# A three-stage block on one core: who makes the inputs of the state scan

## The chip, the core and the metric

The kernel runs on one core of a Trainium2 chip. The metric is the device time of one execution in microseconds (us). The engines named below are TensorE (PE in the profile; PEld is its weight load), VectorE (DVE), ScalarE (ACT), GpSimd (POOL) and SyncE (SP), which here only issues DMAs. All of them work through their own instruction list in order and wait for each other through semaphores. A change within about 0.3% can't be told from no change here.

## The reference, cut to what matters

`x` has 16 batches of 512 tokens with 256 features, all float32. Each batch goes through four residual stages: causal attention with 16 heads of 16 features, a feed-forward layer with a small router over 6 experts, a state-space layer, and the same feed-forward layer again.

```python
x = x + attn(layernorm(x), ...)
x = x + ffn(layernorm(x), ...)
x = x + ssm(layernorm(x), ...)
x = x + ffn(layernorm(x), ...)
```

The state-space layer is where the change is made. Per feature `d` and state `n` (16 states) it runs a recurrence over the 512 tokens:

```python
delta = softplus(xc @ Wd.T + bd);  Bm = xc @ Wb.T;  Cm = xc @ Wc.T
decay = exp(A * dt);  inp = dt * xt * bt     # per state n
h = decay * h + inp
y = sum over n of h * ct
```

## The kernel before, in words

A batch is held with features on the 128 partitions in two halves (C = 2 halves of 128 features) and the 512 tokens along the free dimension. With `u = dt * xc` (both halves, 128x1024), state `n` of batch `s` takes one step of this kind:

- SyncE loads row `n` of B, which lies in DRAM as `b_kept`, broadcast to 128 partitions, into one of three places of `b_all` (`load_b`, L759 on). It waits until `inputs` of three steps earlier is done.
- ScalarE makes `dec` with two exponentials (`decays`).
- GpSimd makes `inp` (`inputs`, L1325 on) with two multiplications of 128x512, one per half: L1333 for half 0, L1339 for half 1, both from `u` and `b_all` in SBUF. `dec` and `inp` have two places each, so `inputs` of step `n` waits for scan `n-2`.
- VectorE runs the recurrence over both halves as one scan of 128x1024 (`scan`, L1164), and then `product` (L1172) multiplies the state by row `n` of C, which TensorE has spread over a PSUM bank (`spread_bank`).
- GpSimd adds the product to `y` by a DMA with addition (`add_state`, L1346). For the last two batches TensorE adds in PSUM instead (`sum_y`, L596).

Only in the last batch is it otherwise already: there TensorE spreads row `n` of B over `pv_bank` (L585), VectorE makes half 1 from it directly behind the scan before (`half_of_inputs`, L1145), and GpSimd makes half 0 alone.

Beside these steps VectorE takes the maxima of the attention scores from two PSUM banks (L1030, L1033, L1035; 40 of them in each batch), normalises heads (L1057, L1059), adds residuals (L1080, L1088), makes silu (L1128), `dt` and `u` (L1136, L1138), the gated y (L1178) and the router (L1096 to L1122). TensorE makes the scores twice (L392, L394 for the maxima; L415, L417 for the exponentials), the products with the values (L440) and all projections.

The order of work is written out by hand. Each engine loops over `now` from START to STOP; a batch has a frame of 80 slots. The tables PE_AT, ACT_AT, DVE_AT, POOL_AT and SP_AT give for each piece of work the slot, counted from its batch's frame, at which an engine takes it up; `due` turns a slot into a batch. A slot is a place in an engine's list and no time: what an engine does is set by the order and the waits. All batches have the same places. Several batches are under way at once, since a batch runs from slot -114 to slot 285 of its frame: the scans of one batch lie beside the attention of a batch two frames later. The last two batches' scans therefore lie behind the end of the attention work.

On each engine the work beside the scans keeps its place in the loop: on VectorE a slot's maximum comes first, then `side_work`, then scans, then products.

Of the kernel before, what the change touches and what calls it, by code (L numbers as in the profile page):

```python
# [56 lines left out]
def hybrid_block(nc, x, norm_w, wqk_t, bqk_c, wv_t, bv, wo_t, bo, conv_w, conv_b, wd_t, bd, wbc_t,  # L57
# [37 lines left out]
    PE_AT = {"res": (-29, -34), "xn": (-76, -74), "qk00": (-55, -51, -47), "qk01": (-47, -45, -43),  # L95
# [6 lines left out]
             "sum": (165, 177, 182, 189, 189, 192, 200, 209, 211, 211, 219, 224, 224, 232, 235, 242)}  # L102
    BANK = {"res": (1, 1), "xn": (0, 0), "qk00": 0, "qk01": 1, "v": (1, 0), "qk10": 0, "qk11": 1, "ao": (0, 1),
            "x1": (1, 1), "turn0": (1, 1), "low0": 1, "hw0": 0, "up0": (0, 1), "xs": (0, 1), "conv": (0, 1),
            "gate": (0, 1), "bc": 1, "dt": (0, 0), "x3": (1, 0), "turn1": (0, 1), "low1": 1, "hw1": 0, "up1": (0, 1)}
    ACT_AT = {"res": (-28, -34), "square_f": 100, "square_s": 124, "square_l": 251, "norm_f": 103, "norm_s": 129,
# [5 lines left out]
              "decays": (154, 165, 169, 170, 170, 176, 187, 190, 197, 197, 204, 216, 218, 219, 219, 225)}  # L112
    DVE_AT = {"gated": 249, "add_x3": (250, 251), "in0": 112, "in1": 265, "out0": 116, "out1": 271,
              "add_up1": (277, 277), "add_x1": (92, 97), "add_up0": (122, 124), "silu": 140, "delta": 153,
              "stats_q": -114, "finish": -7, "heads": 26,
              "scan": (158, 169, 169, 171, 181, 183, 191, 195, 200, 204, 210, 217, 219, 224, 225, 227),
              "product": (161, 170, 174, 178, 182, 186, 194, 198, 201, 209, 215, 217, 222, 225, 232, 235)}
    POOL_AT = {"rsqrt_f": 91, "rsqrt_s": 128, "rsqrt_q": -110, "rsqrt_l": 241, "low": (116, 262),
               "inputs": (147, 152, 152, 152, 162, 167, 180, 180, 196, 204, 205, 210, 220, 221, 221, 225),
               "add": (160, 152, 165, 174, 180, 185, 191, 202, 205, 209, 214, 220, 221, 225, 225, 227)}  # L120
    SP_AT = {"parts": (-41, 1), "load_x": -112, "store_b": 151, "store": 285, "stack": (-29, -30, -29), "maxima": -4,
             "load_b": (152, 155, 156, 164, 169, 169, 175, 180, 194, 199, 208, 208, 211, 215, 215, 227)}
    ctx = ExitStack()
    with ctx:
# [115 lines left out]
        def has(b):  # L240
            return 0 <= b < NB
# [4 lines left out]
        def due(now, at):  # L246

            a, rest = divmod(now - at, FRAME)
            return a if rest == 0 and has(a) else -1

        def group(now, at):

            g, rest = divmod(now - at, HALF)
            return g if rest == 0 and 0 <= g < NQ else -1
# [65 lines left out]
        def _(pe):  # L320
# [257 lines left out]
            def spread_b(s, n):  # L578

                if s == NB - 1:  # L580
                    if n == 0:
                        pe.wait_ge(heads_done.sem, heads_done.at(NQ - 1))
                        pe.wait_ge(side["bc"].free, side["bc"].at("bc", s, 2))
                    pe.wait_ge(b_used.sem, b_used.at(0, n))
                    mm(pv_bank[:, :], onehot[:, n:n + 1].to_broadcast([3 * NC, P]), bcs[:, s % 2, :],  # L585
                       start=True, stop=True).then_inc(b_ready.sem, 1)
# [116 lines left out]
        def _(sp):  # L703
# [317 lines left out]
        def _(dve):  # L1021
# [118 lines left out]
            def half_of_inputs(n):  # L1140

                if n == 0:
                    dve.wait_ge(u_done.sem, u_done.at(NB - 1))
                dve.wait_ge(b_ready.sem, b_ready.at(0, n + 1))
                V.tensor_tensor(inp[:, n % 2, 1, :], pv_bank[:, :], u[:, 1, :], ALU.mult).then_inc(b_used.sem, 1)  # L1145

            def scan(s, n):
                k = NS * s + n
                old_s, old_n = divmod(k - HC, NS)
                if s == NB - 1 and n == 0:  # L1150
                    half_of_inputs(0)
# [13 lines left out]
                if s == NB - 1 and n + 1 < NS:  # L1165
                    half_of_inputs(n + 1)
# [125 lines left out]
        def _(pool):  # L1292
# [142 lines left out]
```

## Time and profile before

| | us |
|---|---|
| median of three runs | 2019.69 |
| lowest and highest of them | 2017.47, 2022.86 |
| the profiled execution, its own time | 2012.02 |
| its span from first to last instruction | 2010.2 |
| VectorE busy in the span | 1697.4 |
| TensorE busy in the span | 1791.8 |
| GpSimd busy in the span | 1163.8 |

The profile page gives busy time of each engine and groups of instructions. A group's line has its line number, engine, operation, what it writes and reads with shapes, the count, and behind the bar its busy time with the mean in ns; behind the next bar the idle time of that engine just before the group and what ended it. Busy time of an engine in a stretch counts overlapping instructions once. The answer by stretch of time gives the same busy times for any stretch, and the timeline lists one engine's instructions in order: start, duration, line. The duration of an instruction that is held while it runs contains the hold.

### The profile page before, as it was taken

The page shows a single profiled execution, that of the slowest core. Times are in us where ns is not written, and L with a number is a line of the kernel's source. Part 1 is how long each engine was busy: PE and PEld are TensorE (multiplying, and loading weights), DVE is VectorE, ACT ScalarE, POOL GpSimd, SP SyncE. Part 2 cuts the span into 40 slices and gives each one's busy share as a digit, 9 for nine tenths or more (in the row PEclk, how much of TensorE's full clock was granted, in tenths as well). Part 3 has the DMA queues.
Part 4 walks back from the last instruction along what each step waited for, and adds up shares of the span by engine and source line. Part 5 has one row for each costly group of instructions (what it writes and reads, how often), then busy time and mean ns, then how long its engine had stood idle before and what let it go on. Part 6 is the DMA issues. An engine that isn't in the chain of part 4 may idle for free.

```text
span 2010.2 us, 33547 instructions
## 1 busy us (share of the span) xinstructions
PE 1791.8 (89%) x11380; PEld 1109.9 (55%) x11380; DVE 1697.4 (84%) x2584; ACT 1408.9 (70%) x2724; POOL 1163.8 (58%) x933
## 2 busy tenths in 40 slices
PE   5889898999899898989999998999999898878775
PEld 3456464646566564746556565646565564535333
DVE  4444789999898989989999999989899999977783
ACT  2465768787785868777786968687886868675531
POOL 2000556676676666676676666666667666667430
PEclk9899989999999999999999999999999999989887
DMA  4322477766767676767768776866768776641110
GB/s 121 90 65 59 110 163 155 179 149 156 160 142 172 148 172 154 171 146 155 165 142 179 163 171 147 179 147 161 158 146 176 158 167 142 148 102 56 40 58 10
DMA packets 186091, 275.41 MB, mean 137 GB/s; under 512 B 33809, under 2 KB 125762, under 8 KB 185922
## 3 DMA queue, kind: packets, MB, share of 16 engines
q1 hardware_dynamic: 155682, 163.17, 31.5%
q0 software_dynamic: 30240, 110.11, 29.1%
q8 instruction: 91, 1.49, 0.3%
q14 instruction: 78, 0.64, 0.1%
HBM read 128.49 MB, written 34.08 MB: 81 GB/s over the span
## 4 chain that ended last, share of the span: by engine, by line
PE 36%; DVE 17%; DMA 15%; ACT 12%; issue 8%; POOL 7%; SPq 4%; POOLq 0%; DVEq 0%; ACTq 0%
PE bank L331 8%; DVE hc L1164 6%; DMA y<-hc 5%; PE bank L538 5%; DMA sk<-qk_parts 5%; SPq L748 3%; POOL inp L1333 3%; DMA out<-X 3%; PE bank L392 3%; PE bank L415 3%; PE bank L341 2%; PE bank L440 2%; PE bank L596 2%; POOL inp L1339 2%; PE bank L325 2%
## 5 line engine op out<-in xcount | busy, mean ns | idle before, releaser
L1164 DVE TENSOR_TENSOR_SCAN hc<-dec,inp 128x1024 f32<-128x1024 f32 x256 | 647.1, 2535 | 44.6 <-POOL inp L1339 13.8
L1333 POOL TENSOR_TENSOR inp<-u,b_all 128x512 f32<-128x512 f32 x256 | 445.9, 1742 | 207.2 <-DVE hc L1164 102.0
L812 ACT ACTIVATE pt<-bank 128x512 f32<-128x512 f32 x640 | 378.1, 596 | 121.8 <-PE bank L417 118.3
L1339 POOL TENSOR_TENSOR inp<-u,b_all 128x512 f32<-128x512 f32 x240 | 387.0, 1612 | 18.8
L928 ACT ACTIVATE dec<-dt,a_neg 128x511 f32<-128x511 f32 x512 | 340.1, 719 | 53.3 <-DVE hc L1164 53.3
L1346 POOL DMA_DIRECT2D y<-hc x210 | 185.5, 883 | 304.2 <-DMA y<-hc 196.2
L392 PE MATMUL bank<-sk,sq 96*128 96x512 bf16 (+3 forms) x1024 | 272.7, 305 | 49.1 <-DMA sk<-qk_parts 34.3
L1172 DVE TENSOR_TENSOR hc<-hc,bank 128x1024 f32<-128x1024 f32 x242 | 293.1, 1211 | 16.6 <-PE bank L575 15.5
L415 PE MATMUL bank<-sq,sk 98*128 98x512 bf16 (+3 forms) x1024 | 271.1, 303 | 8.0 <-ACT pt L812 7.5
L1033 DVE TENSOR_REDUCE mall<-bank 128x1 f32<-128x512 f32 x256 | 173.7, 678 | 62.2 <-PE bank L394 62.1
L1035 DVE TENSOR_REDUCE mall<-bank 128x4 f32<-128x512 f32 x256 | 173.7, 678 | 44.8 <-PE bank L394 44.8
L394 PE MATMUL bank<-mask_qk,ident_bf 128*128 128x128 bf16 x1024 | 194.5, 222 | 0.0
L417 PE MATMUL bank<-mask_kq,ident_bf 128*128 128x128 bf16 x1024 | 194.3, 221 | 0.0
L392 PEld LDWEIGHTS bank<-sk,sq 96*128 96x128 bf16 x1024 | 100.9, 99 | 158.6 <-issue 44.6
L440 PE MATMUL bank<-pt,v_sb 128*32 128x512 f32 (+3 forms) x2048 | 179.3, 446 | 0.8 <-ACT pt L812 0.8
L845 ACT ACTIVATE parts<-bank,bqk 128x512 bf16<-128x512 f32 x192 | 130.2, 688 | 42.6 <-PE bank L331 28.2
L331 PE MATMUL bank<-xt_q,wqk 128*128 128x512 f32 x256 | 125.4, 613 | 16.6 <-ACT bcs L908 15.8
L415 PEld LDWEIGHTS bank<-sq,sk 98*128 98x128 bf16 x1024 | 101.5, 99 | 68.0 <-ACT pt L812 17.4
L394 PEld LDWEIGHTS bank<-mask_qk,ident_bf 128*128 128x128 bf16 x1024 | 101.6, 99 | 45.9 <-issue 26.5
L1311 POOL TENSOR_TENSOR rs<-va,half 128x4 f32<-128x4 f32 x64 | 69.8, 1091 | 88.1 <-DVE ng L1075 84.0
L417 PEld LDWEIGHTS bank<-mask_kq,ident_bf 128*128 128x128 bf16 x1024 | 101.8, 99 | 31.4 <-issue 22.6
L575 PE MATMUL bank<-bcs,onehot 96*128 96x512 bf16 x256 | 98.9, 386 | 20.5 <-DVE hc L1172 20.4
(171 smaller groups left out, 3416.0 us busy)
## 6 DMA issues: line engine op xcount, KB each, us to landing
y<-hc POOLq DMA_DIRECT2D x210, 512.0 KB, 5.4
b_all<-b_kept SPq DMA_DIRECT2D x256, 256.0 KB, 4.4
qk_parts<-parts SPq DMA_DIRECT2D x96, 256.0 KB, 3.2
sq<-qk_parts SPq DMA_DIRECT2D x384, 64.0 KB, 3.7
sk<-qk_parts SPq DMA_DIRECT2D x384, 64.0 KB, 3.8
X<-in_x SPq DMA_DIRECT2D x16, 512.0 KB, 7.7
out<-X SPq DMA_DIRECT2D x16, 512.0 KB, 5.2
sq<-hlt SPq DMA_DIRECT2D x256, 2.0 KB
```

Of the source, the lines that this page charges most:

```text
L331: last = mm(dst[:, :], w[:, c, g * P:(g + 1) * P], src[:, c, :], start=(c == 0), stop=(c == C - 1))
L392: mm(dst[:, o:o + n], sq[0:KS, slot, h, qb * P:(qb + 1) * P], sk[0:KS, slot, h, 0:n], start=True, stop=False)
L394: return mm(dst[:, o + n - P:o + n], ident_bf[:, :], mask_qk[:, :], start=False, stop=True)
L415: mm(dst[:, o:o + n], sk[:, slot, h, kb * P:(kb + 1) * P], sq[:, slot, h, kb * P:T], start=True, stop=False)
L417: return mm(dst[:, o:o + P], ident_bf[:, :], mask_kq[:, :], start=False, stop=True)
L440: last = mm(pv_bank[VW * i:VW * (i + 1), kb * P:T], values_of(a, kb, first + i), pt[:, n % PT, at:at + T - kb * P], start=start, stop=stop ...
L812: A(pt[:, n % PT, :], score_bank[unit % 2][:, :], ACT.Exp).then_inc(exp_done.sem, 1)
L928: last = A(dec[:, n % 2, c, 1:T], dt[:, c, 1:T], ACT.Exp, scale=a_neg[:, c, n:n + 1])
L1164: V.tensor_tensor_scan(h, d, v, 0.0, ALU.mult, ALU.add).then_inc(scan_done.sem, 1)
L1172: V.tensor_tensor(hc[:, k % HC, :, :] if n or s >= LATE else y[:, s % 2, :, :], hc[:, k % HC, :, :], spread_bank[:, None, :].to_broadcast( ...
L1333: first = G.tensor_tensor(inp[:, n % 2, 0, :], u[:, 0, :], b_all[:, k % 3, :], ALU.mult)
L1339: G.tensor_tensor(inp[:, n % 2, 1, :], u[:, 1, :], b_all[:, k % 3, :], ALU.mult).then_inc(inp_ready.sem, 1)
```

## The change

VectorE makes half 1 of `inp` in every batch, not only in the last. In batches 0 to 14 it reads the row of B from `b_all` in SBUF, the same place that GpSimd reads for half 0; the last batch still takes it from `pv_bank`. It stands, as before in the last batch, directly behind the scan before it. GpSimd keeps half 0 only. The scan waits for both. `load_b` waits for both readers of the place that it fills. All places in the five tables are new, and batch 0, batch 14 and batch 15 get tables of their own (OWN), chosen by KIND in `due`. The numbers of operations other than the moved half are unchanged, and BANK gets a few other assignments.

```diff
+    KIND = [1 if a == 0 else max(a - NB + 4, 0) if a >= NB - 2 else 0 for a in range(NB)]
...
         def due(now, at):
-            a, rest = divmod(now - at, FRAME)
-            return a if rest == 0 and has(a) else -1
+            for kind, place in enumerate(at):
+                a, rest = divmod(now - place, FRAME)
+                if rest == 0 and has(a) and kind == KIND[a]:
+                    return a
+            return -1
...
                 sp.wait_ge(inp_ready.sem, inp_ready.at(old_s, old_n + 1))
+                sp.wait_ge(b_used.sem, b_used.at(old_s, old_n + 1))
...
-            def half_of_inputs(n):
+            def half_of_inputs(s, n):
+                k = NS * s + n
                 if n == 0:
-                    dve.wait_ge(u_done.sem, u_done.at(NB - 1))
-                dve.wait_ge(b_ready.sem, b_ready.at(0, n + 1))
-                V.tensor_tensor(inp[:, n % 2, 1, :], pv_bank[:, :], u[:, 1, :], ALU.mult).then_inc(b_used.sem, 1)
+                    dve.wait_ge(u_done.sem, u_done.at(s))
+                if s == NB - 1:
+                    dve.wait_ge(b_ready.sem, b_ready.at(0, n + 1))
+                    rows = pv_bank[:, :]
+                else:
+                    dve.wait_ge(b_loaded[k % 3].sem, b_loaded[k % 3].at(k // 3))
+                    rows = b_all[:, k % 3, :]
+                V.tensor_tensor(inp[:, n % 2, 1, :], rows, u[:, 1, :], ALU.mult).then_inc(b_used.sem, 1)
...
-                if s == NB - 1 and n == 0:
-                    half_of_inputs(0)
+                if n == 0:
+                    half_of_inputs(s, 0)
...
-                if s == NB - 1:
-                    dve.wait_ge(b_used.sem, b_used.at(0, n + 1))
+                dve.wait_ge(b_used.sem, b_used.at(s, n + 1))
...
-                if s == NB - 1 and n + 1 < NS:
-                    half_of_inputs(n + 1)
+                if n + 1 < NS:
+                    half_of_inputs(s, n + 1)
...
-                first = G.tensor_tensor(inp[:, n % 2, 0, :], u[:, 0, :], b_all[:, k % 3, :], ALU.mult)
-                if s == NB - 1:
-                    first.then_inc(inp_ready.sem, 1)
-                else:
-                    first.then_inc(pool_own.sem, 1)
-                    pool.wait_ge(pool_own.sem, pool_own.one())
-                    G.tensor_tensor(inp[:, n % 2, 1, :], u[:, 1, :], b_all[:, k % 3, :], ALU.mult).then_inc(inp_ready.sem, 1)
+                G.tensor_tensor(inp[:, n % 2, 0, :], u[:, 0, :], b_all[:, k % 3, :], ALU.mult).then_inc(inp_ready.sem, 1)
```

Of the tables, the rows of the usual batches for scans, products, inputs and loads of B:

```diff
-              "scan": (158, 169, 169, 171, 181, 183, 191, 195, 200, 204, 210, 217, 219, 224, 225, 227),
-              "product": (161, 170, 174, 178, 182, 186, 194, 198, 201, 209, 215, 217, 222, 225, 232, 235)}
+              "scan": (157, 167, 170, 171, 179, 184, 190, 194, 201, 204, 210, 216, 219, 223, 228, 230),
+              "product": (163, 170, 174, 178, 182, 189, 195, 199, 201, 207, 215, 218, 221, 225, 231, 236)}
...
-               "inputs": (147, 152, 152, 152, 162, 167, 180, 180, 196, 204, 205, 210, 220, 221, 221, 225),
+               "inputs": (142, 152, 152, 152, 164, 167, 176, 184, 193, 194, 201, 202, 214, 218, 218, 221),
...
-             "load_b": (152, 155, 156, 164, 169, 169, 175, 180, 194, 199, 208, 208, 211, 215, 215, 227)}
+             "load_b": (152, 152, 154, 165, 165, 172, 181, 185, 190, 198, 201, 207, 211, 212, 212, 213)}
```

## Rows read from the trace of the kernel before

**Rows 1.** The page: span, and the engines' busy time, share and instruction count.

```profile
span 2010.2 us, 33547 instructions
...
PE 1791.8 (89%) x11380; PEld 1109.9 (55%) x11380; DVE 1697.4 (84%) x2584; ACT 1408.9 (70%) x2724; POOL 1163.8 (58%) x933
```

**Rows 2.** Busy time by stretch: length, PE, PEld, DVE, ACT, POOL, clock, DMA.

```profile
0.00:213.50 213.50, 174.70 (x1170) 104.76 (x1170) 94.94 (x249) 109.75 (x205) 18.53 (x34) 0.96 0.30 83
213.50:1782.90 1569.40, 1450.57 (x9640) 912.21 (x9640) 1445.37 (x2154) 1207.42 (x2343) 1049.92 (x830) 0.99 0.72 158
1782.90:2010.20 227.30, 166.48 (x570) 92.98 (x570) 157.10 (x183) 91.69 (x178) 95.33 (x69) 0.86 0.16 46
```

**Rows 3.** Groups of VectorE instructions between 213.5 and 1782.9 us.

```profile
L1164 DVE TENSOR_TENSOR_SCAN hc<-dec,inp 128x1024 f32<-128x1024 f32 x224 | 568.1, 2544 | 36.1 <-ACT dec L928 11.0 <-issue 10.5 <-POOL inp L1339 10.2
L1172 DVE TENSOR_TENSOR hc<-hc,bank 128x1024 f32<-128x1024 f32 x209 | 253.1, 1211 | 3.0 <-PE bank L575 2.1
L1035 DVE TENSOR_REDUCE mall<-bank 128x4 f32<-128x512 f32 x220 | 149.0, 677 | 26.6 <-PE bank L394 26.6
L1033 DVE TENSOR_REDUCE mall<-bank 128x1 f32<-128x512 f32 x219 | 148.1, 676 | 14.4 <-PE bank L394 14.3
L1030 DVE TENSOR_REDUCE mall<-bank 128x2 f32<-128x512 f32 x110 | 74.6, 678 | 7.6 <-PE bank L394 7.6
L1088 DVE SCALAR_TENSOR_TENSOR X<-bank,X 128x256 f32<-128x256 f32 x164 | 62.4, 418 | 7.9 <-PE bank L522 7.9
...
L1128 DVE SCALAR_TENSOR_TENSOR xc<-sp_t,xc 128x1024 f32<-128x1024 f32 x14 | 22.9, 1634 | 0.4 <-ACT xc L891 0.4
...
L1138 DVE TENSOR_TENSOR u<-dt,xc 128x1024 f32<-128x1024 f32 x14 | 17.1, 1225 | 0.5
```

**Rows 4.** Waits of VectorE from 1782.9 us to the end: total us, times, longest.

```profile
DVE red L1096 <- ACT low L871: 14.0, 1, 14.0
DVE X L1080 <- PE bank L522: 13.6, 5, 8.0
```

**Rows 5.** Timeline of VectorE in the last batch: start, duration, instruction.

```profile
1951.32 0.67 DVE L1145 TENSOR_TENSOR inp<-bank,u 128x512 f32<-128x512 f32 x1
1951.90 1.21 DVE L1172 TENSOR_TENSOR hc<-hc,bank 128x1024 f32<-128x1024 f32 x1
```

**Rows 6.** Groups of GpSimd instructions between 213.5 and 1782.9 us.

```profile
L1333 POOL TENSOR_TENSOR inp<-u,b_all 128x512 f32<-128x512 f32 x224 | 393.8, 1758 | 154.1 <-DVE hc L1164 70.9 <-DVE u L1138 67.0 <-POOL inp L1339 9.5
...
L1346 POOL DMA_DIRECT2D y<-hc x208 | 183.7, 883 | 294.8 <-DMA y<-hc 194.8 <-DVE hc L1172 78.1 <-issue 10.9
```

**Rows 7.** GpSimd's second multiplication: count, ns min/median/max, first and last start.

```profile
L1339 POOL TENSOR_TENSOR inp<-u,b_all x240: 1261/1272/3346, 216.1 to 1873.4; 128x512 f32<-128x512 f32 x120
```

**Rows 8.** Timeline around 637 us: one scan of VectorE, two multiplications of GpSimd.

```profile
637.43 3.31 DVE L1164 TENSOR_TENSOR_SCAN hc<-dec,inp 128x1024 f32<-128x1024 f32 x1 [0.77 <-ACT dec L928]
...
637.03 1.55 POOL L1333 TENSOR_TENSOR inp<-u,b_all 128x512 f32<-128x512 f32 x1
638.66 3.16 POOL L1339 TENSOR_TENSOR inp<-u,b_all 128x512 f32<-128x512 f32 x1
```

**Rows 9.** Timeline around 1795 us: VectorE, then GpSimd; x2 merges two scans.

```profile
1794.75 1.53 DVE L1178 SCALAR_TENSOR_TENSOR y<-gate,y 128x1024 f32<-128x1024 f32 x1 [1.68 <-DMA y<-hc]
1796.21 5.54 DVE L1164 TENSOR_TENSOR_SCAN hc<-dec,inp 128x1024 f32<-128x1024 f32 x2
...
1795.28 2.13 POOL L1339 TENSOR_TENSOR inp<-u,b_all 128x512 f32<-128x512 f32 x1
```

**Rows 10.** The loads of B rows: who waited for them, and time to landing.

```profile
POOL inp L1333: 8.4, 2
...
DMA to landing us min/median/max: 3.0/4.4/8.4
```

More of the change, by code:

```diff
@@ L118, in hybrid_block @@
[L118 to L122 removed]
+    PE_AT = {"res": (-30, -34), "xn": (-74, -74), "qk00": (-56, -50, -48), "qk01": (-48, -45, -42),
[6 rows of a table added]
+             "sum": (160, 171, 180, 186, 187, 187, 205, 207, 207, 207, 212, 226, 227, 232, 233, 236)}
@@ new lines, in hybrid_block @@
+    SP_AT = {"parts": (-45, 0), "load_x": -112, "store_b": 151, "store": 284, "stack": (-30, -29, -31), "maxima": -8,
+             "load_b": (152, 152, 154, 165, 165, 172, 181, 185, 190, 198, 201, 207, 211, 212, 212, 213)}
+    OWN = {
[8 rows of a table added]
+                   "sum": (154, 169, 178, 182, 184, 192, 195, 206, 206, 211, 222, 227, 228, 236, 236, 236)},
+            "ACT": {"res": (-37, -36), "square_f": 100, "square_s": 125, "norm_f": 102, "norm_s": 129, "norm_q": -95,
[4 rows of a table added]
+                   "decays": (152, 163, 165, 170, 171, 171, 184, 186, 188, 191, 203, 211, 215, 215, 220, 228)},
+            "DVE": {"gated": 242, "add_x3": (248, 249), "in0": 110, "in1": 263, "out0": 111, "out1": 263,
+                   "add_up1": (276, 276), "add_x1": (91, 94), "add_up0": (123, 120), "delta": 156, "stats_q": -105,
+                   "scan": (159, 166, 168, 170, 179, 184, 190, 191, 201, 207, 211, 213, 217, 224, 228, 232),
+                   "product": (162, 166, 169, 180, 185, 192, 196, 200, 202, 212, 215, 215, 218, 224, 230, 236)},
+            "POOL": {"rsqrt_f": 87, "rsqrt_s": 114, "rsqrt_q": -116, "rsqrt_l": 238, "low": (99, 265),
+                   "inputs": (138, 143, 150, 154, 159, 173, 174, 183, 189, 197, 199, 206, 209, 214, 217, 219),
+                   "add": (160, 151, 164, 177, 183, 184, 190, 193, 206, 207, 216, 217, 218, 219, 219, 225)},
+            "SP": {"parts": (-48, -1), "load_x": -107, "store": 285,
+                   "load_b": (151, 156, 158, 164, 164, 172, 172, 185, 190, 194, 201, 211, 211, 212, 218, 219)},
+        },
[8 rows of a table added]
+                   "sum": (166, 174, 178, 183, 188, 198, 206, 207, 210, 210, 222, 224, 225, 236, 238, 238)},
+            "ACT": {"res": (-28, -40), "square_s": 128, "square_l": 255, "norm_f": 102, "norm_s": 132,
[5 rows of a table added]
+                   "decays": (154, 164, 170, 171, 172, 176, 186, 191, 194, 198, 203, 214, 214, 214, 225, 225)},
+            "DVE": {"gated": 240, "add_x3": (247, 247), "in0": 111, "in1": 265, "out0": 114, "out1": 267,
+                   "add_up1": (278, 279), "add_x1": (94, 92), "add_up0": (124, 125), "silu": 142, "delta": 157,
+                   "stats_q": -110,
+                   "scan": (162, 167, 170, 171, 180, 186, 191, 197, 199, 205, 208, 215, 220, 223, 229, 233),
+                   "product": (164, 169, 172, 174, 183, 190, 192, 199, 204, 206, 210, 217, 222, 229, 232, 236)},
+            "POOL": {"rsqrt_f": 99, "rsqrt_s": 127, "rsqrt_q": -105, "rsqrt_l": 238, "low": (113, 259),
+                   "inputs": (144, 150, 151, 151, 159, 168, 182, 185, 186, 207, 207, 209, 218, 218, 218, 223),
+                   "add": (160, 162, 163, 177, 186, 188, 190, 196, 197, 204, 204, 212, 227, 231, 232, 232)},
+            "SP": {"parts": (-38, 4), "load_x": -114, "store_b": 149, "store": 287,
+                   "load_b": (154, 155, 156, 161, 166, 172, 178, 183, 195, 199, 201, 201, 207, 208, 221, 221)},
+        },
[8 rows of a table added]
+                   "sum": (172, 178, 178, 181, 187, 191, 197, 205, 205, 211, 220, 227, 228, 232, 239, 242)},
+            "ACT": {"res": (-32, -31), "square_f": 100, "square_l": 247, "norm_f": 105, "norm_s": 132,
[5 rows of a table added]
+                   "decays": (158, 172, 172, 173, 174, 177, 184, 196, 202, 214, 217, 221, 224, 231, 234, 238)},
+            "DVE": {"gated": 236, "add_x3": (251, 255), "in1": 267, "out0": 117, "out1": 274, "add_up1": (276, 279),
+                   "add_x1": (95, 93), "add_up0": (121, 124), "silu": 140, "delta": 157, "stats_q": -107,
+                   "scan": (162, 166, 171, 173, 177, 184, 188, 192, 198, 205, 208, 214, 220, 224, 227, 232),
+                   "product": (163, 167, 172, 173, 181, 184, 192, 199, 201, 207, 208, 219, 223, 225, 229, 234)},
+            "POOL": {"rsqrt_f": 104, "rsqrt_s": 128, "rsqrt_q": -109, "rsqrt_l": 234, "low": (109, 260),
+                   "inputs": (146, 151, 151, 151, 152, 161, 166, 182, 189, 190, 197, 202, 212, 216, 216, 222),
+                   "add": (160, 162, 174, 185, 185, 187, 190, 197, 210, 217, 225, 225, 228, 228, 230, 232)},
+            "SP": {"parts": (-36, 8), "store_b": 161, "store": 275,
+                   "load_b": (164, 164, 164, 165, 165, 179, 180, 190, 199, 201, 204, 208, 208, 220, 221, 232)},
+        },
+    }
@@ new lines, in hybrid_block, with by_batch @@
+    KIND = [1 if a == 0 else max(a - NB + 4, 0) if a >= NB - 2 else 0 for a in range(NB)]
+    def by_batch(engine, usual):
+        rows = [{**usual, **OWN[k].get(engine, {})} if k else usual for k in range(4)]
+        return {key: tuple(zip(*(row[key] for row in rows))) if isinstance(usual[key], tuple) else
+                tuple(row[key] for row in rows) for key in usual}
+    PE_AT, ACT_AT, DVE_AT, POOL_AT, SP_AT = (by_batch(engine, usual) for engine, usual in (
+        ("PE", PE_AT), ("ACT", ACT_AT), ("DVE", DVE_AT), ("POOL", POOL_AT), ("SP", SP_AT)))
```

24 lines of the change are left out of this document (12 added, 12 removed), and 60 rows, old and new, of tables (ACT_AT, OWN, PE_AT).

## The prediction

> **What bounds the kernel now.** I read the page first, for the shares of the engines. TensorE is busy for 89% and VectorE for 84% of a span of 2010.2 us, GpSimd for 58% [rows 1]. These are means over stages, so I cut the span where VectorE makes `u` of a batch: the first `u` starts at 213.5 us, that of batch 14 at 1782.9 us. Between these lie 14 batch periods of 112.1 us with the whole scan work of batches 0 to 13. In that stretch VectorE is busy for 1445.4 of 1569.4 us (92.1%) and idle for 124.0 us; TensorE for 1450.6 us (92.4%); GpSimd for 1049.9 us (66.9%) [rows 2]. Before it VectorE is busy for 94.9 of 213.5 us, behind it for 157.1 of 227.3 us [rows 2]. So two engines share the bound of the long stretch, and GpSimd, which the change relieves, isn't one of them.
>
> The groups of that stretch say what ends VectorE's idle time [rows 3]. Ahead of the maxima it waits for TensorE's scores (26.6, 14.4 and 7.6 us, 48.6 in all), ahead of the scans 36.1 us (of which GpSimd's half 1 ends only 10.2), ahead of the residual additions 7.9 us. That makes 92.6 of the 124.0 us. The other 31.4 us are short gaps between small instructions that depend on each other. The reader should see that at most 10.2 us are put down to the GpSimd instruction that goes, and that VectorE has only 124.0 us to take new work into.
>
> **Part 1: the added multiplication.** The trace has its twin in the last batch, 0.67 us long, but the product behind it starts 0.58 us after it, because neighbours on VectorE overlap [rows 5]. The new ones read the row from SBUF instead of PSUM. The rows to compare are a 1024-wide multiplication of two SBUF operands, 1.225 us, and the one with a PSUM operand, 1.211 us [rows 3]: 0.014 us more for 1024, and so about 0.01 us for 512. I take 0.59 us (0.58 to 0.67 as bounds). In the stretch there are 14 x 16 = 224 of them: 132 us (130 to 150). That alone is more than the 124.0 us of idle time; VectorE would need 1445 + 132 = 1577 us in a stretch that now takes 1569 us, with not one gap left. Batch 14 gets 16 more (9.4 us) in the end stretch, where VectorE has 70.2 us idle [rows 2]; its longest waits there are for the router and for the projections of the last feed-forward layer (14.0 and 13.6 us [rows 4]). I cost these at nothing; without that cover they are 9 us.
>
> The Trainium skill, in "VectorE: DVE Perf Modes", section "The TRN2 errata — SBUF-src ops pay a fixed extra latency per instruction", gives a float32 `tensor_tensor` of N elements (N+151) cycles at 0.96 GHz, which is 0.69 us as an estimate from that page, and its section "The DRAIN you can't avoid" has the next instruction start only when the pipe is empty. By that 224 would cost 155 us, 23 us more than I take; the trace disagrees on the second point, since the neighbour starts 0.09 us before the end of the 0.67 us.
>
> **Part 2: the removed multiplication.** GpSimd loses 224 instructions in the stretch whose median is 1.27 us [rows 7], 285 us and more of its queue. As GpSimd waits there 294.8 us for its own DMA additions and their products anyway, and 154.1 us ahead of the first multiplication [rows 6], its queue isn't what ends last. Directly the change gives back at most the 10.2 us of scans that waited for it, and I count these within the idle time below.
>
> **Part 3: the holds.** VectorE instructions with two SBUF inputs and GpSimd's multiplications don't run at the same time. A scan takes 2.29 us undisturbed. The one at 637.43 took 3.31: GpSimd's first multiplication had begun at 637.03 and ended at 638.58, and GpSimd's second, begun at 638.66 inside the scan, took 3.16 us instead of 1.27, until 1.08 us behind the scan's end [rows 7, 8]. Whoever comes second waits. The scans of the stretch take 568.1 us where 224 x 2.29 = 513 are due, and the 14 silus 22.9 us where 14 x 1.225 = 17.2 are due [rows 3]: 61 us of VectorE's busy time are such holds. The change pulls at this in both directions. Half as many GpSimd multiplications meet the scans. But the new VectorE multiplication has two SBUF inputs too and stands directly behind a scan, where a GpSimd instruction that was held by the scan goes first: at 1795.28 GpSimd's began inside an instruction of VectorE and waited, and of the two scans behind, which should take 4.5 us together, 5.54 were needed, a hold of 1.07 us for the next VectorE instruction [rows 9]. Bound from below: the 61 us vanish. Bound from above: to the 61 us come holds of the new instruction. GpSimd's first multiplications took 393.8 us; alone they would take 1.27, or 1.55 behind a DMA issue as at 637.03, some 1.41 on average, 316 us, so 78 us of waiting; at about 1.2 us each (waits lie between 0 and 1.9) some 65 of the 224 waited for VectorE, and 65 x 1.07 = 70 us. I take the middle: the scans keep half of their holds, the new instructions get about half of the 70, together about the 61 of now, no change.
>
> The Trainium skill, in "Advanced Engine Details and Errata", section "Mode Summary", says that GpSimd instructions and VectorE instructions in a two-port mode block each other. Its "GPSIMD Engine Reference", section "Key points", adds instructions with two SBUF inputs, and that is what the rows show; by the first page alone the moved half would be free of holds.
>
> **Part 4: the idle time that is left.** When VectorE has more to do than it has time, what it waits for comes earlier relative to it. The 31.4 us of gaps between dependent instructions stay. Of the 92.6 us of real waits I keep a little over a quarter, 25 us, since maxima and scores pass through two banks only and TensorE is itself 92% busy. Idle time 56 us (bounds 31 and 124).
>
> **Part 5: the new waits.** VectorE now waits for the row of B before the next scan's turn, directly behind the scan before. Behind it on VectorE are queued products and maxima, and TensorE waits for the maxima. Now the rows are in time: GpSimd waited twice for one, and landing takes 4.4 us [rows 10]. A row is asked for when step n-3 is done, two scans (and so usually over 10 us) before its new reader comes. I cost it at nothing. The wait added to `load_b` on SyncE's queue is for an instruction that stands before the scan of step n-3, while the same queue waits for GpSimd's half of that step already; behind it stand the stacking of heads and the maxima rows, and TensorE waits for these. Nothing, for the same reason. The places move no work between engines.
>
> **Part 6: the edges.** The order of batches 0, 14 and 15 is new. In the last 227.3 us TensorE is busy for 166.5 and VectorE for 157.1 us [rows 2], so there are gaps, but most belong to chains of one batch through several engines, which no place shortens. The change can take at most what waits behind something avoidable: I take 14 us (bounds 0 and 30). At the front TensorE is busy for 174.7 of 213.5 us; a few us, in the 14.
>
> **The sum.** The stretch: 1445 + 132 + 0 + 56 = 1633 us, against 1569: +64. Edges: -14. The profiled execution took 2012.0 us, so 2062. The median of the runs is 7.7 us above the profiled time, so 2070 us, 2.5% above 2019.7.
>
> **The rivals.**
>
> Rival 1, faster: the holds vanish. If the new order keeps GpSimd's one multiplication away from the scans (it is triggered by a scan's end and takes 1.27 us, and the new multiplication and a product cover 1.8 us), VectorE gets 61 us back: 1445 - 61 + 132 + 56 = 1572, +3. Edges -14 to -30: 1993 to 2009, about 2001. For it: the holds come from scans placed side by side (slots 169, 169, 171), now 170, 171 with a product between. Against: it needs nearly all of them gone. It decides from holds below about 30% of today's, with the edges at their better end.
>
> Rival 2, much slower: the new instruction is caught behind waiting GpSimd instructions as often as the trace has such waits. All of the 70 us instead of half of it, and the scans keep their 61: about 66 us on top, 2136. For it: rows 9. Against: GpSimd's queue is shorter, so its instructions start nearer to their trigger.
>
> Rival 3: late rows. If VectorE reaches one row per batch before it has landed, one landing each, 14 x 4.4 = 62 us, 2132. Against: rows 10.
>
> Rival 4: the places do more than the sum says, so that idle time falls to the 31 us and some of the holds go, which leaves the moved work just covered: 2013 to 2035.
>
> That the instruction isn't what it seems (0.67 us instead of 0.59) adds 18 us and stays in the forecast.
>
> **How the numbers follow.** Forecast 0.52 (its own range 2035 to 2105), rival 1 0.20, rival 4 0.12, rival 2 0.11, rival 3 0.05. Faster by over 0.3% is below 2013.6: rival 1, 0.20. Within 0.3%, up to 2025.7: the larger part of rival 4, 0.07. Slower: 0.73. The range leaves out the better end of rival 1 and the upper halves of rivals 2 and 3, some 0.2 in all: 2000 to 2120.
>
> **What would show it.** Right: the distance between the `u` of batches 0 and 14 at about 1633 us with VectorE busy for over 96% of it; 240 new instructions of 0.67 to 0.7 us in the median; VectorE's waits for the scores well below 48 us; TensorE waiting longer for the maxima; holds (scan time above 2.29 us each, plus the new instruction's above its median) near 61 us. Wrong: scan mean near 2.3 us (rival 1); the new instruction's mean well above 0.9 us (rival 2); VectorE idle ahead of it until a DMA of `b_all` (rival 3); a last stretch shorter than 195 us, which would mean that I undervalued the places.

## The result and the profile after

The changed kernel takes 2053.45 us (median of four runs, 2052.3 to 2057.4) where the kernel before takes 2018.58 us (median of four). The ratio is 1.0177, with a 95% interval of 1.0149 to 1.0205. The profiled execution of the changed kernel took 2057.44 us.

The page after, same parts as [rows 1]:

```profile
span 2055.6 us, 33966 instructions
...
PE 1804.4 (88%) x11336; PEld 1119.1 (54%) x11380; DVE 1814.3 (88%) x2824; ACT 1403.2 (68%) x2724; POOL 723.5 (35%) x693
```

GpSimd lost 440 us of busy time and VectorE gained 117, and the span grew. Cut where VectorE makes the `u` of batches 0 and 14, as in [rows 2] (length, then PE, PEld, DVE, ACT, POOL, clock, DMA):

```profile
0.00:208.50 208.50, 171.99 (x1171) 105.25 (x1175) 97.13 (x251) 109.54 (x205) 18.61 (x34) 0.97 0.30 85
208.50:1835.40 1626.90, 1467.17 (x9594) 920.23 (x9634) 1555.12 (x2378) 1201.68 (x2341) 640.06 (x607) 0.98 0.74 152
1835.40:2055.60 220.20, 165.26 (x571) 93.64 (x571) 162.04 (x197) 91.98 (x180) 64.81 (x52) 0.88 0.16 46
```

The long stretch grew by 57.5 us, to 116.2 us per batch. The front got 5.0 us shorter and the end 7.1 us. VectorE is now busy for 95.6% of the long stretch (92.1% before), idle for 71.8 us instead of 124.0. Its groups there, answering [rows 3]:

```profile
L1264 DVE TENSOR_TENSOR_SCAN hc<-dec,inp 128x1024 f32<-128x1024 f32 x224 | 537.3, 2399 | 6.6 <-DVE inp L1246 3.0 <-DMA y<-hc 2.5 <-ACT dec L1023 0.6
L1272 DVE TENSOR_TENSOR hc<-hc,bank 128x1024 f32<-128x1024 f32 x210 | 254.0, 1210 | 11.8 <-PE bank L669 11.0 <-issue 0.2
L1246 DVE TENSOR_TENSOR inp<-b_all,u 128x512 f32<-128x512 f32 x224 | 177.3, 791 | 0.0
L1130 DVE TENSOR_REDUCE mall<-bank 128x4 f32<-128x512 f32 x219 | 149.6, 683 | 4.5 <-PE bank L488 4.5
L1128 DVE TENSOR_REDUCE mall<-bank 128x1 f32<-128x512 f32 x218 | 148.0, 679 | 4.0 <-PE bank L488 3.7
L1125 DVE TENSOR_REDUCE mall<-bank 128x2 f32<-128x512 f32 x110 | 75.1, 683 | 4.7 <-PE bank L488 4.6
```

L1246 is the new instruction. Its line shows no idle time ahead of it: VectorE never waited for a row of B. The waits for the scores (the three reductions) fell from 48.6 to 12.8 us and those ahead of the scans from 36.1 to 6.6. The other side of it is in TensorE's waits for VectorE in the same stretch. Before, the longest for a maximum was 6.5 us in total and that for the product 10.3 us:

```profile
PE bank L486 <- DVE mall L1128: 39.3, 40, 2.2
PE bank L669 <- DVE hc L1272: 35.5, 18, 3.4
```

VectorE, which waited for TensorE before, now makes it wait. TensorE's granted clock in the stretch was 0.98, before it was 0.99. In the four longest stretches of the runs below (1656 us and more) it was 0.96 or 0.97. But move_only_pool_thin, whose stretch is as long as this one (1624.8 us), had 0.99, so the lower clock isn't needed for such a length. How much it adds elsewhere no run here separates.

Duration of the new instruction in the stretch (min, median, max in ns):

```profile
L1246 DVE TENSOR_TENSOR inp<-b_all,u x224: 657/666/2570, 210.7 to 1828.2; 128x512 f32<-128x512 f32 x112
```

Its median is that of its twin in the last batch, 0.67 us [rows 5]; the mean is 0.79, so 28 us of the 177.3 are holds (177.3 - 224 x 0.666). The scans' holds fell from 55 to 24 us (537.3 - 224 x 2.29).

A hold of the new instruction looks like this. First VectorE, then GpSimd around 683 us of the changed kernel:

```profile
680.86 2.29 DVE L1264 TENSOR_TENSOR_SCAN hc<-dec,inp 128x1024 f32<-128x1024 f32 x1 [0.20 <-DVE inp L1246]
683.07 2.57 DVE L1246 TENSOR_TENSOR inp<-b_all,u 128x512 f32<-128x512 f32 x1
...
682.90 0.87 POOL L1440 DMA_DIRECT2D y<-hc  x1 [2.80 <-DMA y<-hc]
683.51 1.57 POOL L1433 TENSOR_TENSOR inp<-u,b_all 128x512 f32<-128x512 f32 x1
```

GpSimd issued a DMA at 682.90 and had a multiplication queued behind it. VectorE's instruction, begun at 683.07, took 2.57 us instead of 0.67. It ended at 685.64, 0.56 us behind the end of GpSimd's multiplication (685.08). Its own work takes 0.67 us, so nearly all of it was done only then, although the multiplication's recorded start, 683.51, is the later one.

### The profile page after: what moved, and what is told of

Same layout as the page of the kernel before. It is cut to its first block, busy times and chain, and to the rows that moved or that the text cites. A ratio compares the mean times of both kernels' runs of the same rounds, so it can differ in the third digit from the quotient of the medians.

```text
span 2055.6 us, 33966 instructions
## 1 busy us (share of the span) xinstructions
PE 1804.4 (88%) x11336; PEld 1119.1 (54%) x11380; DVE 1814.3 (88%) x2824; ACT 1403.2 (68%) x2724; POOL 723.5 (35%) x693
## 4 chain that ended last, share of the span: by engine, by line
DVE 40%; PE 27%; DMA 13%; issue 9%; ACT 6%; POOL 3%; SPq 1%; DVEq 0%; another core or an unknown queue 0%; POOLq 0%; ACTq 0%
DVE hc L1264 14%; DMA y<-hc 8%; DVE hc L1272 5%; DVE inp L1246 4%; PE bank L425 4%; PE bank L615 3%; DVE mall L1128 3%; DVE mall L1130 3%; PE bank L632 3%; DMA X<-in_x 2%; PE bank L534 2%; PE bank L486 2%; PE bank L509 2%; PE bank L435 2%; DVE mall L1125 2%
## 5 line engine op out<-in xcount | busy, mean ns | idle before, releaser
L1264 DVE TENSOR_TENSOR_SCAN hc<-dec,inp 128x1024 f32<-128x1024 f32 x256 | 614.4, 2400 | 12.4 <-ACT dec L1023 6.2
L1433 POOL TENSOR_TENSOR inp<-u,b_all 128x512 f32<-128x512 f32 x256 | 392.5, 1533 | 391.5 <-DVE hc L1264 237.6
L1246 DVE TENSOR_TENSOR inp<-b_all,u 128x512 f32<-128x512 f32 x240 | 190.4, 793 | 0.0
L425 PE MATMUL bank<-xt_q,wqk 128*128 128x512 f32 x256 | 136.9, 672 | 2.6 <-ACT bcs L1003 1.9
L632 PE MATMUL bank<-xs_t,taps 128*128 128x512 f32 x256 | 119.7, 611 | 0.1
```

The lines of the kernel that those rows point to most:

```text
L1246: V.tensor_tensor(inp[:, n % 2, 1, :], rows, u[:, 1, :], ALU.mult).then_inc(b_used.sem, 1)
L1264: V.tensor_tensor_scan(h, d, v, 0.0, ALU.mult, ALU.add).then_inc(scan_done.sem, 1)
```

## The experiments

My theory: the time went to VectorE, which has 131 us more to do in a stretch with 124 us of idle time; holds at the port that it shares with GpSimd come on top; the places take some 12 us off the edges. Rival P: the new places cost the time and the moved half is free. Rival H: holds alone carry the difference. The ratio is to runs of before on the same chip at the same time (medians 2020.9, 2016.0 and 2018.9 us beside the three groups of experiments). Differences in us below are of medians. Between kernels of different groups the ratios give up to 8 us less: 35 instead of 41 us for places_only against the changed kernel, 23 instead of 30 for late_half, 113 instead of 121 for move_only_pool_thin against move_only. The argument rests on none of these gaps.

| kernel | median us | ratio (95%) | stretch us | VectorE busy in it |
|---|---|---|---|---|
| before | 2018.6 | 1 | 1569.4 | 1445.4 |
| changed | 2053.5 | 1.0177 (1.0149 to 1.0205) | 1626.9 | 1555.1 |
| places_only | 2094.5 | 1.0350 (1.0307 to 1.0394) | 1657.7 | 1469.7 |
| move_only | 2193.5 | 1.0837 (1.0787 to 1.0888) | 1739.2 | 1664.2 |
| late_half | 2083.0 | 1.0290 (1.0249 to 1.0331) | 1656.0 | 1538.6 |
| half_as_wide | 2018.5 | 0.9992 (0.9960 to 1.0024) | 1588.2 | 1488.7 |
| more_work | 2086.7 | 1.0343 (1.0314 to 1.0372) | 1664.9 | 1592.4 |
| after_pool_thin | 2018.6 | 1.0005 (0.9988 to 1.0021) | 1592.1 | 1502.3 |
| move_only_pool_thin | 2072.9 | 1.0278 (1.0248 to 1.0309) | 1624.8 | 1515.1 |
| before_pool_thin | 1995.1 | 0.9898 (0.9863 to 0.9933) | 1554.6 | 1372.4 |
| places_only_pool_thin | 1985.8 | 0.9841 (0.9810 to 0.9873) | 1560.1 | 1375.6 |
| edges_only | 2075.3 | 1.0294 (1.0265 to 1.0322) | | |
| move_in_batch_14 | 2023.8 | 1.0010 (0.9985 to 1.0035) | | |

**Undo one part: places_only and move_only.** places_only is the kernel before with the changed kernel's tables and `due`. Each cut below shows the edit against the changed kernel:

```diff
-                G.tensor_tensor(inp[:, n % 2, 0, :], u[:, 0, :], b_all[:, k % 3, :], ALU.mult).then_inc(inp_ready.sem, 1)
+                first = G.tensor_tensor(inp[:, n % 2, 0, :], u[:, 0, :], b_all[:, k % 3, :], ALU.mult)
...
+                    G.tensor_tensor(inp[:, n % 2, 1, :], u[:, 1, :], b_all[:, k % 3, :], ALU.mult).then_inc(inp_ready.sem, 1)
```

> The changed kernel's places (usual tables and the own ones of batches 0, 14 and 15), but GpSimd makes both halves in batches 0 to 14 as before. My theory (the 2% are VectorE time: 224 instructions of 0.58 us in a stretch with 124 us of idle time, less some holds; the places give about 12 us at the edges): the stretch between the u of batches 0 and 14 falls from 1627 back to 1560 to 1580 us, the edges stay 12 us shorter, so 1998 to 2020 us. Rival (the new places cost the time, the moved half is free): it stays at 2040 us or more.

Measured: 2094 us, 41 us more than with the move. My theory fails here: it had 1998 to 2020 us. Rival P's number (2040 or more) is met, and the new places do cost time by themselves, but its other half is wrong, since the move isn't free in these places: it saves time. The new places without the move are worse than either kernel. VectorE's busy time fell to 1469.7 us, 24 more than before, mostly holds on small router instructions, and it is idle for 188 us. Its longest waits in the stretch:

```profile
DVE hc L1258 <- DMA y<-hc: 46.9, 24, 7.1
DVE mall L1129 <- PE bank L488: 21.9, 27, 5.1
DVE hc L1258 <- POOL inp L1433: 21.6, 12, 5.1
```

Scans wait for the additions to `y`, which GpSimd issues in order behind its multiplications, and for GpSimd's half. These two waits, 68.5 us together, were 14.4 us before.

move_only is the changed kernel with the five tables, BANK and `due` of before:

```diff
-            for kind, place in enumerate(at):
-                a, rest = divmod(now - place, FRAME)
-                if rest == 0 and has(a) and kind == KIND[a]:
-                    return a
-            return -1
+            a, rest = divmod(now - at, FRAME)
+            return a if rest == 0 and has(a) else -1
```

> The places of the kernel before, but VectorE makes half 1 in every batch. My theory: the stretch grows by 58 to 75 us and the edges don't get shorter: 2065 to 2090 us, more than the changed kernel. Rival (the new places cost the time): 2015 to 2030 us.

Measured: 2193 us, over 100 us more than my upper value. This is where rival P falls, which had 2015 to 2030. The move costs 173 us in the old order and gains 41 us (35 by the ratios) in the new one. VectorE's busy time grew by 219 us, not by 132, and two lines show where it went:

```profile
L1170 DVE TENSOR_TENSOR_SCAN hc<-dec,inp 128x1024 f32<-128x1024 f32 x224 | 625.6, 2793 | 12.7 <-DVE inp L1152 8.4 <-ACT dec L929 3.9 <-issue 0.3
...
L1152 DVE TENSOR_TENSOR inp<-b_all,u 128x512 f32<-128x512 f32 x224 | 178.6, 797 | 0.0
```

The scans' holds doubled, to 112 us (625.6 - 513); the new instruction has 29. So the amount of holds depends on the order. The amount of the prediction's rival 2 was reached in the old order, but on the scans and not on the new instruction, where rival 2 had it. One place of a hold, VectorE and then GpSimd:

```profile
696.27 0.66 DVE L1152 TENSOR_TENSOR inp<-b_all,u 128x512 f32<-128x512 f32 x1
697.13 3.08 DVE L1170 TENSOR_TENSOR_SCAN hc<-dec,inp 128x1024 f32<-128x1024 f32 x1 [0.20 <-DVE inp L1152]
...
696.50 1.57 POOL L1339 TENSOR_TENSOR inp<-u,b_all 128x512 f32<-128x512 f32 x1 [1.77 <-issue]
```

The old order has two scans side by side at slot 169. The scan in front sets GpSimd's multiplication going at its end; the new instruction stands between and goes first, so GpSimd runs from its end on, straight into the next scan, which takes 3.08 us. The new places put a product between such scans. That isn't the main part, though. The 45 scans that stand directly behind a new instruction have 41 of the 119 us of scan holds in the whole of move_only. 88 us are on 49 scans that began while GpSimd was issuing a DMA with a multiplication right behind it, as in the last section; in the kernel before this kind made 21 us. Why the old order brings it about so often with the move wasn't tested.

**Take the suspected holds away: four kernels with GpSimd's multiplication cut to 8 columns.** From the third step of batch 0 to the end of batch 14 (the other columns of `inp` keep old values: part of the computation is left out):

```diff
+                w = T if k < 2 or s == NB - 1 else 8
-                G.tensor_tensor(inp[:, n % 2, 0, :], u[:, 0, :], b_all[:, k % 3, :], ALU.mult).then_inc(inp_ready.sem, 1)
+                G.tensor_tensor(inp[:, n % 2, 0, 0:w], u[:, 0, 0:w], b_all[:, k % 3, 0:w], ALU.mult).then_inc(inp_ready.sem, 1)
```

> The changed kernel, but from the third step of batch 0 to the end of batch 14 GpSimd's multiplication makes 8 of 512 columns (work left out), so that it hardly meets VectorE at the port. Holds theory: the 52 us of holds (24 on scans, 28 on the new instruction) go from VectorE's busy time in the stretch, mean scan 2.29 and mean new instruction 0.67. As half_as_wide stopped at 113 us per batch with less VectorE work, TensorE then sets the stretch, so the time falls by 30 to 45 us, to 2010 to 2025. Rival (the cost is the additional work alone, holds are only moved waiting time): less than 15 us fall.

Measured: 2018.6 us, 35 less, VectorE's busy time down by 53 us as the holds theory has it. The two groups that were held:

```profile
L1264 DVE TENSOR_TENSOR_SCAN hc<-dec,inp 128x1024 f32<-128x1024 f32 x224 | 513.1, 2291 | 7.5 <-DMA y<-hc 3.7 <-DVE inp L1246 3.0 <-ACT dec L1023 0.6
...
L1246 DVE TENSOR_TENSOR inp<-b_all,u 128x512 f32<-128x512 f32 x224 | 149.7, 668 | 0.0
```

The cut also shortens GpSimd's queue, but VectorE hardly waited for GpSimd in the changed kernel (0.2 us ahead of the scans). VectorE's idle time rose from 71.8 to 89.8 us, so 18 of the 53 us came back as waits.

> As move_only (places of before, half 1 made by VectorE everywhere), with GpSimd's multiplication 8 columns wide in batches 0 to 14. move_only has some 112 us of holds on its scans and 29 on the new instructions. If the places matter through the port, these go and the kernel comes to where the changed kernel with the same cut comes: 2010 to 2050 us. Rival (the old order is bad with the move for another reason, such as a wait in a queue): it stays above 2120 us.

Measured: 2072.9 us, 121 us less than move_only and VectorE's busy time down by 149 us. So holds are the larger part of what the old order costs with the move, but I expected 2050 at most; the 54 us to after_pool_thin stay. 33 us of them are in the stretch, where VectorE has about the same work in both (1515 and 1502 us) and is idle 20 us longer. About 19 us are at the edges, 446.0 us against 427.4 (span less stretch). What makes the idle time I didn't settle; TensorE's longest wait there, 25.6 us, is for stacked heads.

> The kernel before with both of GpSimd's multiplications 8 columns wide from the third step of batch 0 to the end of batch 14 (work left out). VectorE is then rid of 55 us of holds on scans and of waits for GpSimd. If VectorE's time alone set the 112 us per batch of before, 40 to 60 us go. If TensorE sets a floor near 112 us, as half_as_wide suggests, less than 20 us go.

Measured: 1995.1 us, 21 us less, just beyond the 20 that I gave the floor. VectorE is busy for only 1372 of 1555 us (111.0 us per batch), TensorE for 1442 (92.8%). VectorE waits for the scores for 100 us there:

```profile
DVE mall L1033 <- PE bank L394: 44.4, 36, 2.6
DVE mall L1035 <- PE bank L394: 38.8, 43, 3.3
...
DVE mall L1030 <- PE bank L394: 16.4, 26, 0.8
```

73 us less VectorE work gave 15 us of stretch. In this order about 111 us per batch is what remains when VectorE is light, and VectorE waits for TensorE there, so I take TensorE and its chains as this floor; TensorE's own work was not changed in any run. The kernel before stood just above it, at 112.1. This run also decides rival H. after_pool_thin alone would fit it, since without holds the changed kernel is back at the time of before. But with GpSimd light in both kernels the changed one is still 23 us slower (2018.6 against 1995.1), with under 4 us of holds in either. So holds alone don't carry the difference.

> As places_only (the changed kernel's places, both halves at GpSimd), with both of GpSimd's multiplications 8 columns wide from the third step of batch 0 to the end of batch 14 (work left out). places_only lost 55 us against before's places: scans waited 47 us for the DMA additions to y, which GpSimd issues. If that is GpSimd's longer work in places made for a shorter one (additions issued later), it falls by 60 to 90 us, to the floor that TensorE sets, 2005 to 2035 us. If the new places are simply worse in themselves, it stays at 2050 us or more.

Measured: 1985.8 us, 109 us less than places_only and even below my range. With a loaded GpSimd that makes both halves the new tables are 74 us worse than the old; with a light one they are 9 us better, and the intervals of these two still touch. The edges alone make the difference (424.0 against 438.8 us). The stretch is no shorter than that of before_pool_thin, 111.4 against 111.0 us per batch. So in the steady part the new order has no gain of its own. It only suffers more from GpSimd's load: 98 us of stretch against 15. Its VectorE busy time falls by 94 us with the cut, 57 of them holds on scans and most of the rest on router instructions, while its idle time hardly changes (188.0 and 184.5 us). With GpSimd light the move costs time in either order: 33 us in the new one (2018.6 against 1985.8), 78 us in the old one (2072.9 against 1995.1). What it gains in the new order with a loaded GpSimd is thus GpSimd's relief. The cut takes holds and queue away together, so it doesn't say which of the two the new order bears worse.

**Change the size of VectorE's work: half_as_wide and more_work.**

```diff
+                w = T if s == NB - 1 or k < 2 else T // 2
+                V.tensor_tensor(inp[:, n % 2, 1, 0:w], rows[:, 0:w], u[:, 1, 0:w], ALU.mult).then_inc(b_used.sem, 1)
```

> The changed kernel, but from the third step of batch 0 to the end of batch 14 VectorE's new instruction makes only the first 256 of 512 columns (the other columns of inp keep old values; work left out). It takes 0.27 us less, 238 times: 64 us less VectorE work, 59 of them in the stretch. If VectorE's time sets the stretch, 45 to 64 us go (ratio to before 0.985 to 0.995). If the cost is holds or the additional wait and not the work: under 20 us go (ratio 1.007 or more).

Measured: 35 us less, between my two values. Busy time fell by 66 us, the stretch only by 39, to 113.4 us per batch, and idle time rose to 99.5 us. So VectorE's time counts for a little over half here, still 2.4 us per batch above the 111: the two engines wait for each other over a range, and there is no sharp edge.

```diff
+                if s < NB - 1:
+                    V.tensor_tensor(again[:, :], rows[:, 0:T // 4], u[:, 1, 0:T // 4], ALU.mult)
```

> The changed kernel with one more VectorE multiplication of 128 columns in front of each new one in batches 0 to 14. It adds some 0.18 us (0.58 less 384 columns of 1.04 ns), 224 times in the stretch: 40 us of VectorE work. If VectorE's time sets the stretch, the time grows by 30 to 50 us, to 2085 to 2105 us. If the two per cent came from something else (a wait, the port, a chain through GpSimd) and VectorE had room, it grows by under 15 us.

Measured: 33 us more (1.0343 against 1.0177). VectorE's busy time grew by 37 us and the stretch by 38 us. In this direction nothing cushions it: here VectorE's time is the kernel's time. Of all runs this one needs the fewest assumptions, as it leaves nothing out and keeps the order.

**Move the new instruction: late_half.**

```diff
-                if n == 0:
-                    half_of_inputs(s, 0)
+                if n == 0 or s < NB - 1:
+                    half_of_inputs(s, n)
...
-                if n + 1 < NS:
+                if s == NB - 1 and n + 1 < NS:
```

> The changed kernel, but in batches 0 to 14 VectorE makes half 1 of step n directly ahead of scan n instead of directly behind scan n-1. If the 28 us by which the new instructions exceed 0.666 us each come from GpSimd multiplications that waited through the scan in front and go first at its end, most of them go: VectorE busy 15 to 28 us less in the stretch, 2028 to 2045 us. Rival (the hold only moves, to the scan that now follows directly or to the half in front of it, since GpSimd then runs at the same time as the pair): no change, 2048 to 2060 us.

Measured: 2083 us, 30 more than the changed kernel. Both expectations missed. VectorE's busy time did fall, by 16.5 us: the scans' holds went from 24 to 5.5 us and those of the new instruction from 28 to 19. But a new wait came:

```profile
L1264 DVE TENSOR_TENSOR_SCAN hc<-dec,inp 128x1024 f32<-128x1024 f32 x224 | 518.5, 2315 | 46.8 <-DVE inp L1246 37.5 <-DMA y<-hc 8.1 <-ACT dec L1023 1.2
```

The scan waits for the instruction directly in front of it, 185 times, 0.20 us each in the mean, 37.5 us in all. The waits for scores grew too, from 12.8 to 28.1 us. The place behind the scan before, with other work between, saves that gap.

**The edges: edges_only and move_in_batch_14.** Both have the usual places of before and the half made by VectorE from batch 14 on (`s >= MOVED`, MOVED = NB - 2); edges_only gives batch 0 its own new places as well.

```diff
+    MOVED = NB - 2
+                if n == 0 and s >= MOVED:
+                    half_of_inputs(s, 0)
```

> The places of before, but batch 0 has its own new places and VectorE makes half 1 in batches 14 and 15 only, where it has idle time. If the gain of the edges (12 us in the changed kernel) comes from batch 0's places and the move in batch 14: 3 to 10 us below before (ratio 0.995 to 0.998). If it comes from the own places of the last two batches: no change.

> The kernel before with all its places; VectorE makes half 1 in batches 14 and 15 only. The prediction costed the 16 added instructions of batch 14 at nothing, since VectorE is idle for 70 of the last 227 us. Then the time is that of before within 0.3%, with up to 4 us less since GpSimd is relieved there; if they aren't hidden, up to 9 us more.

edges_only measured 2075 us, 59 more than before, where I expected a small gain. From the `u` of batch 0 to that of batch 2 it takes 278.6 us (218.2 to 496.8) where before takes 223.9; from there on it is as before. So batch 0's own places don't go with the old usual ones around them. Its end, from batch 14's `u` on, is 224.6 us, 3 less than before. move_in_batch_14 measured the time of before (1.0010, 0.9985 to 1.0035). Its stretch from the `u` of batch 14 to the end:

```profile
1790.30:2018.60 228.30, 165.92 (x570) 93.02 (x570) 165.47 (x198) 91.68 (x178) 61.54 (x53) 0.86 0.16 46
```

Against [rows 2] VectorE is busy for 8.4 us more and the stretch is 1.0 us longer: the 16 instructions are hidden there. The edges' gain comes with the new places and not with the move: span less stretch is 440.8 us before, 428.8 in the changed kernel, 429.3 in places_only and 445.6 in move_only. The own places of batches 14 and 15 alone over the old usual ones weren't tried. No kernel that does the whole computation came out below the kernel before.

## Why the prediction was right

The direction and the mechanism were right for this pair of kernels. Forecast were 2070 us and a slowdown of 50 us; measured were 2053.5 and 35. By its own steps:

- **The added work**: 0.59 us each, 132 us. Less what the instruction in front of each already covers (18.3 us), the new instructions hold VectorE for 159.0 us in the stretch, 28 of them holds, so 131. more_work shows that this time is paid in full where the changed kernel stands; half_as_wide shows that less work gives only some 0.6 of it back. So this step was right. The prediction set the Trainium skill ("VectorE: DVE Perf Modes", "The DRAIN you can't avoid") against the trace, but left out that the same paragraph lets a next instruction that isn't held start earlier. So page and trace don't differ on the 0.09 us of overlap. The 0.69 us by the skill's formula is above the 0.666 us measured here.
- **The removed work**: nothing from GpSimd's queue but 10 us. Right in size for this order. But places_only shows what I left out: how much GpSimd's work costs depends on the order. In the new one, taking the half from GpSimd is worth more than VectorE pays for it.
- **The holds**: forecast unchanged at 61 us. With the small router instructions, which I hadn't counted, they were 68 us; now 24 on scans and 28 on the new instruction, about 16 us less. Half of the scans' holds went, as the forecast has it, and its 35 us on the new instruction were 28. The middle was a fair choice in the new order; in the old one (move_only, 141 us) even the bound from above would have been too low by 10 us.
- **The idle time left**: 56 us forecast, 71.8 measured. The waits for scores fell as said, but products waited 11 us for the spread row of C and the statistics 8 us for the loaded x. The prediction put 31.4 us down to gaps between dependent instructions. That was a misreading: at least 8.6 of them were waits too, 3.6 for the loaded x and 2.1 for the row of C among them, and these two grew. Undervalued by 16, and the holds happened to give back 16: that the stretch came out so close is in part luck. The prediction wanted VectorE busy for over 96% of it; measured were 95.6.
- **The sum of the stretch**: 1633 forecast, 1626.9 measured. VectorE's busy time alone was 22 us below its forecast (1555 against 1577), the idle time 16 above.
- **The new waits**: nothing. VectorE had no idle time ahead of the new instruction. GpSimd did wait for rows of B (59.6 us in 11 waits, 8.4 in all before), beside the bound.
- **The edges**: -14 forecast, -12.1 measured. Batch 14's work at nothing is confirmed by move_in_batch_14, in the old places.
- **From the profiled time to the median**: here lies most of the 17 us. The sum gave 2062 for the profiled execution, which took 2057.4. I then added 7.7 us, since the median of before was that much above its profiled run; the changed kernel's median is 4.0 us below its own. A difference between one execution and a median isn't a property to carry over.

Rival 1 (holds vanish) can be priced by after_pool_thin: with all holds gone the kernel comes to 2018.6, the time of before, not the 2001 of the forecast. Its step that fails is the idle time held at 56 us: it was 89.8, so the stretch is 1592 and not 1572 us. That the lighter VectorE waits more for TensorE is the reason that I give. But the stretch is still 32 us above the 1560.1 that the same order reaches in places_only_pool_thin, and TensorE waits for VectorE there too (31.5 and 27.3 us), so TensorE's floor alone isn't it. Rival 4 fails by the idle time as well, 71.8 us where it had 31. Rival 3 (late rows) had no trace at VectorE.

What the forecast missed is that the 35 us aren't the price of the move but of a move and an order together. The move alone costs 173 us, the new order alone 74 us, both together 35 (169, 71 and 36 by the ratios). The prediction's sum adds up work and places apart. My expectations for each alone were worked out in the same way and missed by 74 and 103 us, so that the sum fits the two together is in part luck. What differs between the orders is shown in part: the holds (52 us in the changed kernel, 141 in move_only) and the waits for GpSimd (68.5 us in places_only).

## What to carry to other kernels

When two engines each fill over 90% of a steady stretch, compare the work added to one of them with its idle time there first: here 131 against 124 us pointed to a slowdown. But idle time is not simply free to be filled. With half of the added work the kernel only came back to the time of before, as waits grow when work shrinks. Price the idle time that remains, and try what is left when one engine is made light (here 111 us per batch), since it caps what can be won back. And when a change moves work and order at once, don't read its time as the price of the move: a hand-made order belongs to the durations that it was made for.

## What the runs showed of the hardware

- In these traces a VectorE scan or multiplication with two SBUF inputs and a GpSimd multiplication don't run at the same time; one of them waits. With GpSimd's multiplications cut to 8 columns the scans' holds fell from 24 to under 2 us. The product, a 1024-wide multiplication with one of its two inputs in PSUM, was never held: its 256 instances took 1.19 to 1.22 us in the kernel before and in the changed kernel alike. The Trainium skill ("GPSIMD Engine Reference", "Key points") names this contention, and the trace agrees.
- A hold can come from a GpSimd multiplication whose recorded start is up to 0.5 us later than that of the VectorE instruction it holds, when GpSimd is just issuing a DMA in front of it. Around 642.5 us in the kernel before a scan took 4.13 us:

```profile
642.51 4.13 DVE L1164 TENSOR_TENSOR_SCAN hc<-dec,inp 128x1024 f32<-128x1024 f32 x1
...
642.30 0.88 POOL L1346 DMA_DIRECT2D y<-hc  x1 [0.48 <-DVE hc L1172]
642.90 1.58 POOL L1333 TENSOR_TENSOR inp<-u,b_all 128x512 f32<-128x512 f32 x1
```

  By the records 12 of the 76 scans with a hold over 0.08 us in the kernel before are of this kind (21 us of 64), and 51 of 125 instructions in move_only (92 us of 154). In all of them VectorE's instruction began inside the DMA issue and ended as if its own work had started 0.13 us before the multiplication's end. The DMA issue by itself doesn't hold a scan: the 19 scans of the kernel before that began during one with no other GpSimd instruction in their time took 2.28 to 2.29 us. Whether the multiplication takes the port before its recorded start, or its record is late, isn't shown.
- A VectorE instruction that depends on the one directly in front starts 0.20 us after its end (late_half), while independent neighbours overlap by 0.08 to 0.09 us. By these two figures a dependent pair side by side costs about 0.3 us more than an independent one, an estimate.
